# A routed expert stage: the queue that loads weights first waits for an activation to return from memory

## The reference, cut to what matters

```python
gate = jax.lax.ragged_dot(xs, w_gate, group_sizes)     # rows x 1024 times 1024 x 512
up   = jax.lax.ragged_dot(xs, w_up, group_sizes)
down = jax.lax.ragged_dot(jax.nn.silu(gate) * up, w_down, group_sizes)   # 512 x 1024
routed = (down[unsort].reshape(T, K, H) * tkw[..., None]).sum(axis=1)
```

## Time and profile before

| what | value |
|---|---|
| median of 3 runs | 11616.19 us (11613.81 to 11616.75) |
| the profiled execution's own time | 11656.14 us |
| its span, first to last instruction | 11654.5 us |
| PE busy | 11263.2 us, 97% of the span |
| DVE, ACT, POOL busy | 4582.6, 2893.0, 4356.9 us (39%, 25%, 37%) |
| mean granted TensorE clock | 0.983 of full speed |
| weight pieces loaded within the loop | 168 (28 experts of 6), median 11.8 us from issue to landing |
| PE idle before `pd`, ended by ACT's `a_hi`, from 2830 us on | 74.8 us in 32 waits, the longest 6.6 us |
| PE idle before `pg`, ended by nothing that is recorded, from 2830 us on | 9.3 us in 7 waits |

### The profile page before, as it was taken

The page is one execution under the profiler, slowest core; times in us unless marked ns, Lnnn a source line. Parts: engine busy times, 40 slices in busy tenths (PEclk is TensorE's granted clock), DMA queues, the critical chain, the costliest instruction groups (busy, mean ns, idle before and its releaser), DMA issues.

```text
span 11654.5 us, 205447 instructions
## 1 busy us (share of the span) xinstructions
PE 11263.2 (97%) x49984; PEld 9240.4 (79%) x49985; DVE 4582.6 (39%) x6239; ACT 2893.0 (25%) x3906; POOL 4356.9 (37%) x4236
## 2 busy tenths in 40 slices
PE   8999599998999999999999999999998999999998
PEld 7888377776888888888888878878887787888887
DVE  5777566664232323332323232232334323223222
ACT  1111244442222222222222222222223222122221
POOL 2666432222333333333333333333433333333333
PEclk9999699999999999999999999999999999999999
DMA  5555466764444444454544454454556445444443
GB/s 184 170 171 171 115 171 177 178 173 138 97 117 111 105 98 117 118 135 99 137 98 118 97 154 100 96 134 98 138 137 177 128 98 155 97 97 117 98 96 85
DMA packets 955079, 1485.12 MB, mean 127 GB/s; under 512 B 318626, under 2 KB 621922, under 8 KB 931912
## 3 DMA queue, kind: packets, MB, share of 16 engines
q0 software_dynamic: 212800, 623.06, 25.2%
q1 hardware_dynamic: 357640, 476.85, 13.0%
q10 hardware_dynamic: 384512, 383.85, 11.7%
HBM read 887.22 MB, written 596.15 MB: 127 GB/s over the span
## 4 chain that ended last, share of the span: by engine, by line
PE 66%; DVE 2%; DMA 2%; issue 2%; ACT 1%; DVEq 1%; ACTq 1%; POOL 0%; SPq 0%; POOLq 0%
PE pd L2007 22%; PE pg L66 7%; PE pg L68 7%; PE pg L67 7%; PE pu L68 7%; PE pu L67 7%; PE pu L66 7%; DMA activated<-av 2%; DVE w_lo L1909 2%; DVEq L1589 1%; ACT w_hi L1817 1%; ACT x_hi L1821 0%; ACTq L1589 0%; DMA aq<-activated 0%; DVE aT L1931 0%
## 5 line engine op out<-in xcount | busy, mean ns | idle before, releaser
L1780 POOL DMA_INDIRECT out_rows<-y,idx_s x528 | 864.2, 1637 | 4434.5 <-issue 4424.2
L1772 POOL DMA_INDIRECT xq<-xn_rows,idx_q x2124 | 2141.7, 1008 | 937.2 <-issue 487.5
L1821 ACT ACTIVATE x_hi<-xT 128x1024 fp32r<-128x1024 f32 x530 | 562.9, 1062 | 4576.5 <-DMA activated<-av 4411.6
L66 PE MATMUL pg<-w_hi,x_hi 128*128 128x512 f32 x4224 | 1646.4, 390 | 49.8 <-DVE x_lo L1924 40.3
L66 PE MATMUL pu<-w_hi,x_hi 128*128 128x512 f32 x4224 | 1644.8, 389 | 1.9 <-DVEq L1978 1.4
L67 PE MATMUL pg<-w_lo,x_hi 128*128 128x512 f32 x4224 | 1645.3, 390 | 0.0
L68 PE MATMUL pg<-w_hi,x_lo 128*128 128x512 f32 x4224 | 1645.2, 389 | 0.0
L67 PE MATMUL pu<-w_lo,x_hi 128*128 128x512 f32 x4224 | 1643.3, 389 | 0.0
L68 PE MATMUL pu<-w_hi,x_lo 128*128 128x512 f32 x4224 | 1643.3, 389 | 0.0
L1959 DVE SCALAR_TENSOR_TENSOR av<-pu,scale,sg 128x512 f32<-128x512 f32 x528 | 396.5, 751 | 3030.2 <-PE pu L68 2760.2
L1924 DVE TENSOR_TENSOR x_lo<-xT,x_hi 128x1024 fp32r<-128x1024 f32 x530 | 649.7, 1226 | 1582.9 <-ACT x_hi L1821 1571.7
(11 more groups left out here) (277 smaller groups left out, 14630.7 us busy)
## 6 DMA issues: line engine op xcount, KB each, us to landing
stage<-in_w_all SPq DMA_DIRECT2D x174, 1024.0 KB, 11.8
activated<-av ACTq DMA_DIRECT2D x528, 256.0 KB
aq<-activated ACTq DMA_DIRECT2D x528, 256.0 KB
rep<-steps ACTq DMA_DIRECT2D x192, 512.0 KB
xq<-xn_rows,idx_q POOLq DMA_INDIRECT x2124
xt<-in_x SPq DMA_DIRECT2D x64, 512.0 KB
xn_rows<-xn SPq DMA_DIRECT2D x64, 512.0 KB, 2.7
sxq<-xn_rows SPq DMA_DIRECT2D x256, 128.0 KB
```

Of the source, the lines that this page charges most:

```text
L66: m(dst, hi, whi[:, cols], start=begin, stop=False)
L1772: g.indirect_dma_start(out=xq[q][:, n], out_offset=None, in_=xn_q, in_offset=bass.IndirectOffsetOnAxis(ap=idx_q[q][:, n:n + 1], axis=0))\
L1780: g.indirect_dma_start(out=out, out_offset=bass.IndirectOffsetOnAxis(ap=idx_s[q][:, 0:1], axis=0), in_=y[q][:], in_offset=None, compute_op ...
L1821: a.activation(x_hi[q][:].rearrange("p b (g j) -> p b g j", g=4), xT[:].rearrange("p (g b j) -> p b g j", g=4, b=KH), ACT.Copy).then_inc(x ...
```

## The change

Two lines are added in SP's `tile`, one in each branch that loads weights. Before the value reads and loads of a new expert's pieces, SP waits until `a_loaded` has reached t*16. Each load of an activation raises this semaphore by 16, so at this point the activations of all tiles up to t-1 have come back from memory. The wait stands in an instruction of its own that also counts up `sp_passed`.

```diff
@@ -1725,10 +1725,12 @@
                 wait_past(sp, av_ready, t)
                 load_scale(t + 1, 1 - q)
                 with sp.If(value_of(sp, fresh, t + 2, 1) > 0):
+                    wait_past(sp, a_loaded, t * 16, sp_passed)
                     load(t + 2, (0, 1, 2, 3))
                 with sp.Else():
                     sp.sem_inc(sp_passed, 1)
                 with sp.If(value_of(sp, fresh, t + 1, 1) > 0):
+                    wait_past(sp, a_loaded, t * 16, sp_passed)
                     load(t + 1, (4, 5))
                 with sp.Else():
                     sp.sem_inc(sp_passed, 1)
```

## The result

The changed kernel takes 11656.66 us (median of 6 runs, 11651.98 to 11667.81), the kernel before 11616.47 us (6 runs, 11613.81 to 11623.61). The ratio is 1.0035, 95% interval 1.0025 to 1.0046: slower, by 29 to 53 us. Forecast were 11647 us and +31. Two more comparisons with fresh runs gave 1.0036 (1.0022 to 1.0050) and 1.0029 (1.0019 to 1.0038).

A forecast was written before the change was run, and what follows sets the result against it. PE is busy nearly throughout, so the change acts only through its few waits, clustered behind expert changes. Terms 31.5 + 3 - 3.5 give +31 us, a median of 11647 us; range 11611 to 11672 us.

The forecast's parts named there:

- The wait meets a load that nothing disturbs.: Load of av(t-1) at an expert change: lands at about 5573.3 before any weights move, so the wait gains nothing there.
- SP stands 1.8 us; the pieces leave 1.85 us later.: SP's new wait: stands 1.8 us (1.3 to 2.3), reads not hidden, four loads leave at 5575.1 instead of 5573.25.
- The store's landing follows the weights' issue.: Store of av(t): lands 17.12 to 17.40 us after the weights' issue, so it moves by the whole 1.85 us.
- rival B: Delay hidden: store served between weights' packets, or SP without profiler comes after the landing; 11613 us, chance 0.23.
- 1 us per us.: Chain from the store to PE's products: each microsecond of delay costs 1 us; lower bound 0.78.
- The 17 ordinary changes: 17 of 28 expert changes, weights 4.3 to 5.0 us behind the store of av(t-1): 17 x 1.85 = 31.5 us.
- The four changes where SP came a little later: Forecast for three changes where SP comes later and waits in part: 0.8, 0.2 and 2.0 us, together 3 us.
- How the delay is split over PE's waits: PE at a new expert: pg waits 0.5 us, pu as much, pd a tile later 1.6 to 2 instead of 0.7.
- The slack of 1.35 us: Between the end of w_lo and pg's start: 1.8 us, some 0.45 us signalling, about 1.35 us slack.
- rival C: PE's granted clock falls behind the new waits: 11676 us at all 17 changes, 11661 at half; chance 0.13.
- The one place that gains: At 6844.35 two pieces no longer precede the activation's load; PE's 5.12 us wait becomes about 2.5, saving 3.5 us.
- The wait of the earlier trace stays: At a single-tile expert SP passes the new wait before the collision, so PE's 5.83 us wait stays.

The follow-up runs named there:

- weights earlier: Against the kernel before, without the change's waits: the branch loading pieces 0 to 3 stands ahead of the av_ready wait and scale load; 11615.02 against 11643.24 us, ratio 0.9976.
- larger dose: Against the kernel before: one wait ahead of pieces 0 to 3, until DVE has turned the activation of tile t-1; 11739.47 against 11616.28 us, ratio 1.0107.
- reads first: Against the changed kernel: both waits kept, but SP reads its two numbers before waiting; 11650.08 us against 11643.24 us of the kernel before, ratio 1.0005.

## Why the prediction was right, and where not

- *The wait meets a load that nothing disturbs.* Shown: with the wait, the activation's load is as fast as without (both profiles have it landed before the weights' first byte), so there was nothing to gain there.
- *SP stands 1.8 us; the pieces leave 1.85 us later.* SP stood 2.1 us, and the pieces left 2.0 us later at the change shown (6.56 instead of 4.57) and in the median of the 17 (6.53 instead of some 4.55). The two reads behind the wait are not hidden: 1.5 us without a byte on the engines, and moving them ahead brought the loss from over 30 us down to 7.
- *The store's landing follows the weights' issue.* Right for the change, and only roughly right as a rule. At the change of the earlier trace rows the distance is 17.12 us before, 17.43 after, and 14.91 with a quarter less; the time from the store to its landing grew by 2.3 us as the weights came 2 us later. But with the weights earlier it is 17.1 to 19.5 us and in the larger dose 14.6 to 18.1. The landing comes with the end of the weights' burst, 0.9 to 2.5 us behind their last packet in the versions with 4 MB, and not at a fixed time.
- *Why it does.* The prediction took turns packet by packet to mean that the store gets through between the weights, and gave that to rival B. That reading was wrong. The trace tells packets by queue (packets, MB, share of the 16 engines; q1 has SP's weights, q0 POOL's gathers, q10 ACT's store). In the changed kernel from 5565.5 to 5568.5, behind the store's issue at 5565.14:

```profile
q1 hardware_dynamic: 121, 0.92, 72.3%
q0 software_dynamic: 123, 0.33, 27.6%
```

  No packet of the store moves yet, while alone (issued at 5568.68 in the kernel before) all of its 528 packets, 0.26 MB, lie between 5569 and 5571. In the larger dose, from 5595.5 to 5598.5, behind the store's issue at 5591.91:

```profile
q1 hardware_dynamic: 159, 1.17, 92.6%
q10 hardware_dynamic: 155, 0.08, 8.7%
```

  Here the two queues take turns: 155 packets against 159. The Trainium skill ("DMA: Bandwidth & Descriptors", "Queues, rings and completion order") has each transfer engine go round its queues packet by packet, and the trace agrees. But a packet of the store is 0.5 KB and one of the weights over 7 KB, so in 3 us the store gets 0.08 of its 0.26 MB, and the rest goes when the weights are through. Why its first packet comes more than 3 us behind its issue in these places is not shown. Rival B is out, with its other half too: the five executions of the changed kernel that ran without the profiler are as slow as the one with it.
- *1 us per us.* Tile by tile the traces give the sum directly (averages of three profiles of each kernel, from the tile in which the weights are issued to four tiles later). The 17 ordinary changes cost 32.1 us together, 1.9 us each; forecast were 31.5. The four changes where SP came a little later cost 0.4 to 0.8 us each, 2.2 together (forecast 3, for three of them); the place of the earlier trace rows gives 2.8 us back (3.5). What is left is -3.5 us in other places. Together this is the +28 us of the stage. By version (the last column is the average over the 13 ordinary changes that no expert of a single tile follows at once):

| version | pieces 0 to 3 behind the store of av(t-1), median | store to the issue of its load, median | cost per change |
|---|---|---|---|
| before | 4.6 us | 5.5 us | - |
| weights earlier | 3.0 us | 5.1 us | -0.4 us |
| reads first | 5.4 us | 6.5 us | +0.8 us |
| the change | 6.5 us | 7.6 us | +1.9 us |
| turned activation | 8.9 us | 9.1 us | +5.8 us |

  The cost follows the store's own time more closely than the time of the weights' issue. The versions other than the first and the changed kernel have one profile each. Of the 5.8 us some 1.7 are the clock (an estimate, from the stretch behind the wait of 2.18 us).
- *How the delay is split over PE's waits* was off. Forecast 0.5 at `pg`, 0.5 at `pu`, 1.6 to 2 at `pd`. Measured 0.78, 0.17 and 1.45, and over all changes nearly the whole new waiting is at `pg` (9.3 to 29.5 us). The slack of 1.35 us there was read rightly, but the chain came 2.1 to 2.3 us later and not 1.85; and what `pg` waits, `pu` and `pd` no longer have to, which the split left out. The waits listed grew by 19 us, and the stage by 31. The list counts too little: a product shows as busy for 0.39 us while the next one starts 0.23 us later, so a gap of the list is some 0.16 us short of the real one, and there are 33 more of them. Counted from start to start of PE's products, the pauses of over 0.3 us come to 98.9 us before and 128.1 us after, 29 us more.
- *The clock* (rival C): no. 1.00 behind the new waits at the change shown, and over the stage the lower level lasts 81 to 86 us against 76 to 90 before. It did come at the larger dose.
- *The one place that gains*: `pd` waits 1.79 us instead of 5.12, as forecast (2.5), though 2.20 us came back at `pg`.
- *The wait of the earlier trace rows stays*, since SP passes the new wait long before: shown.
- The size: +40 us (29 to 53) against +31. What the stage shows, 28 us on average and 31 on one chip, is the forecast. The terms of the sum hold one by one within 1 us; only the 3.5 us of small gains elsewhere are not in it. Against the 40 us of the first comparison the forecast is 9 us short, and what those are is open as said.

## What to carry to other kernels

A wait that should keep two transfers apart has to be for the transfer that they collide with: here it awaited one that was nearly back, and pushed 4 MB by 2 us into the next one, whose way to PE had next to no slack. Look for the transfer whose landing ends last, and see what was issued ahead of it: issuing the burst earlier, or making it smaller, gave 28 and 34 us, both together 51. A small transfer made of small packets gets little beside a burst of large ones, even on a queue of its own. And put a wait behind the reads and address work that don't need it.

## What was not expected

What is issued behind a 4 MB burst ends with the burst: a store of 256 KB that takes 2.3 us alone took 4.7, 5.4, 7.7 and 8.5 us as the burst was issued 12.8, 11.8, 9.8 and 6.6 us ahead of it.

PE's waits for one cause can move to another place without growing there: `pd <- a_hi` fell from 72.6 to 68.7 us in the slower kernel.
